# Macaron block on one core: the first pass starts after a short setup, the other weight transposes stand inside its steps, and the slot products are summed in PSUM one step later

## The chip, the core and the metric

The kernel runs on one core of one Trainium2 chip. The metric is the device time of one execution in microseconds (us). The engines are the tensor engine (PE; PEld is its weight load), the vector engine (DVE), the activation engine (ACT), GpSimd (POOL) and the sync engine (SP), whose queue issues nearly all transfers (SPq in the rows). Everything is float32.

## What is computed

The input x has the shape (2, 4096, 512). Two half-weight "slot" feed-forward blocks (with the same weights) stand around one gated delta-rule attention:

```
x = x + 0.5 * ffn(layernorm(x))
x = x + attn(layernorm(x))
x = x + 0.5 * ffn(layernorm(x))

ffn(x):                                # x already normalised; S = 64 slots, D = 512
  S      = slot_init * slot_scale
  h      = gelu([x, mean(S)] @ w1.T + b1)                # 1024 -> 256
  logits = (h @ w2.T + b2) / (|tau| + 0.1)               # 256 -> 64 slots
  alpha  = softmax over the 8 largest logits, 0 elsewhere
  gi     = (alpha.T @ x) / (sum_t alpha + 1e-8)          # over all 4096 tokens of a batch
  h_new  = GRU(gi, S; wih, whh, bih, bhh)
  return (alpha @ (h_new @ wv.T + bv)) @ wo.T + bo
```

The sum over all tokens of `alpha.T @ x` must be complete before the first block can return anything, so the kernel needs a pass over all tokens before the attention pass can begin.

## The kernel before

The tokens are cut into NT = 32 tiles of 128 tokens per batch row; a step works on one tile of each of the B = 2 rows (b = 0, 1). Each engine has its own instruction stream in program order, and semaphores (`wait_ge`, `then_inc`) are all that ties them; the order within a stream is written out by hand. The program has five parts.

**Setup.** SP loads the constants and the weights. 31 weight blocks of 128 rows (`jobs`: w1, w2, wo, wih, whh; one more job turns the slots `hs`) are loaded into four ring buffers, turned by four transposes each on PE (L625) and moved from PSUM by ACT (L1109, L1112). Then PE makes the 12 products of the slots with whh (`gh_part`, L315), which DVE adds to `gh` (L1528), the mean of the slots (L634) from which DVE makes the bias `h_bias` (L1531 to L1535), and the product of wv with wo (L639, `voT_at`) with its bias (L643, `bvo`). DVE also makes the masks (L1513 to L1524), scales w_out (L1503) and adds biases (L1504), spreads bv (L1508). All of it is done before `ready` is given (after L1546). The turned wih and the product are also stored in DRAM scratch (`wih_dram`, `vo_dram`) for the second use.

**First pass** (`pass1_pe`, `pass1_dve`, ACT's loop of `route_*`). Per step n, DVE takes the moments of tile n + 2 (L1552, L1554), POOL makes the reciprocal deviation (L1337, L1332), DVE normalises (L1563); PE turns the tile (L649), ACT moves it (L1116), PE computes the hidden layer (`route_hidden`, L662), ACT applies gelu (L1126), PE makes the logits (`route_logits`, L672), DVE finds the top 8 (`top_of`, L1569 to L1575), ACT takes exp (L1132), DVE makes alpha (`weights_of`, L1580 to L1584), PE multiplies alpha with the tile and with a column of ones (`route_slots`, L683, L684), turns alpha (L686) for ACT to move (L1137) and SP to store. DVE adds the two products to `slotacc` (`route_sums`, L1596, L1597). The logits of step n wait for ACT's move of step n - 1 (`aT`), the products of step n for DVE's sum of step n - 1 (`sacc`). Each batch row has one buffer for x (`xin`), loaded again when the normalisation has read it.

**First middle** (`mid`, `mid_dve_part`): the GRU, then the slot values `sv`. **Main pass**: first block's output, attention, routing of the second block, three steps deep; this takes most of the time and the change leaves it as it is. **Second middle and tail**: the GRU again, then the second block's output is added to the 32 tiles kept on the chip (L1921) and stored.

## Time and profile before

| | us |
|---|---|
| median of 3 runs | 3365.73 (3364.14 to 3366.76) |
| the profiled execution, its own time | 3365.4 |
| span of its instructions | 3363.2 |
| setup, to the issue of the first load of x | 82.5 |
| from there to the first transpose of the first middle | 320.1 |
| from there to the first transpose of the second middle | 2886.4 |
| from there to the end | 74.2 |
| PE busy over the span | 2867.8 (85%) |
| mean granted PE clock | 0.938 |

The profiled execution's own time is 2.2 us longer than its span and agrees with the median of the runs within 0.4 us. The middle rows come from looking at the trace in windows; the first two together, 402.6 us, are what the change touches.

### The profile page before, as it was taken

What the parts mean: (1) busy time and instruction counts of PE and PEld (TensorE: products, weight loads), DVE (VectorE), ACT (ScalarE), POOL (GpSimd) and SP (SyncE); (2) the same over time, 40 slices, a digit from 0 to 9 for tenths busy, and PEclk for the clock granted to TensorE, in tenths of its full rate; (3) what the DMA queues carried; (4) which work ended last, traced back from release to release, by engine and by line L of the source; (5) the groups of instructions that cost most, each with busy time, mean ns of one, the idle gap of its engine ahead of it and who ended that gap; (6) DMA issues with size and microseconds to landing.
All of it is one profiled execution on the core that took longest, in us unless ns stands there. A gap on an engine that the chain in (4) does not pass through costs nothing.

```text
span 3363.2 us, 121625 instructions
## 1 busy us (share of the span) xinstructions
PE 2867.8 (85%) x52954; PEld 2001.7 (60%) x52954; DVE 1965.6 (58%) x5371; ACT 948.1 (28%) x1662; POOL 1211.3 (36%) x1576
## 2 busy tenths in 40 slices
PE   6888778889898888989888888889898888989857
PEld 4666546566665666656566666666665666656643
DVE  2777645556565565656566665666666656655535
ACT  2555412222222222222222222222222222222210
POOL 0111034444443444434443434344443444434400
PEclk9999989999999998999999999999999999999968
DMA  7211112222221221112222222222222221212157
GB/s 253 68 64 58 45 33 53 54 54 54 54 54 48 54 52 37 50 46 53 54 54 54 54 54 54 54 54 54 54 54 54 54 54 52 54 44 54 47 196 288
DMA packets 365984, 225.07 MB, mean 67 GB/s; under 512 B 277584, under 2 KB 294032, under 8 KB 365456
## 3 DMA queue, kind: packets, MB, share of 16 engines
q1 hardware_dynamic: 356240, 200.51, 21.7%
q10 hardware_dynamic: 9216, 16.78, 1.3%
q8 instruction: 421, 6.90, 0.9%
q14 instruction: 107, 0.88, 0.1%
HBM read 125.49 MB, written 74.97 MB: 60 GB/s over the span
## 4 chain that ended last, share of the span: by engine, by line
PE 49%; DVE 33%; issue 10%; DMA 4%; SPq 2%; ACT 0%; POOL 0%; DVEq 0%; POOLq 0%; ACTq 0%
DVE blk L1764 12%; DVE blk L1766 11%; PE psum L752 8%; PE psum L926 4%; PE psum L835 4%; PE psum L906 4%; PE psum L883 4%; PE psum L853 4%; PE psum L893 4%; DMA xin<-in_L_attn_x_dram 3%; PE psum L797 3%; PE psum L820 2%; PE psum L866 2%; PE psum L954 2%; PE psum L746 2%
## 5 line engine op out<-in xcount | busy, mean ns | idle before, releaser
L752 PE MATMUL psum<-w_kvqg,xnT 128*128 128x512 f32 x1536 | 727.1, 607 | 3.8 <-DVE gt L1689 1.9
L1332 POOL TENSOR_TENSOR sm<-sm,half 128x1 f32<-128x1 f32 (+1 forms) x384 | 517.5, 1348 | 491.5 <-DVE sm L1791 204.9
L1764 DVE TENSOR_TENSOR blk<-blk 128x30 f32<-128x30 f32 (+14 forms) x960 | 377.8, 394 | 83.9 <-issue 51.9
L752 PEld LDWEIGHTS psum<-w_kvqg,xnT 128*128 128x128 f32 x1536 | 270.6, 191 | 253.7 <-issue 226.2
L1766 DVE TENSOR_TENSOR blk<-blk 128x30 f32<-128x30 f32 (+14 forms) x960 | 377.7, 393 | 33.0
L797 PE MATMUL psum<-xnT,w_kvqg 128*128 128x128 f32 x2048 | 300.5, 309 | 0.0
L797 PEld LDWEIGHTS psum<-xnT,w_kvqg 128*128 128x128 f32 x2048 | 290.2, 224 | 16.6 <-issue 16.6
L1354 POOL TENSOR_SCALAR sm<-sm 128x1 f32<-128x1 f32 x64 | 14.5, 227 | 788.1 <-DVE sm L1674 788.1
L926 PE MATMUL psum<-w_out,gate 128*128 128x512 f32 x512 | 269.3, 651 | 2.7 <-issue 1.2
L1782 DVE STREAM_TRANSPOSE st<-psum 128x128 f32<-128x128 f32 x256 | 80.8, 316 | 278.6 <-PE psum L906 278.4
L1162 ACT ACTIVATE xn<-xc,sm 128x512 f32<-128x512 f32 x64 | 52.1, 813 | 655.1 <-POOL sm L1358 655.1
L906 PE MATMUL psum<-qg,st 32*32 32x64 f32 x8192 | 181.0, 219 | 34.3 <-issue 31.1
L906 PEld LDWEIGHTS psum<-qg,st 32*32 32x32 f32 x8192 | 140.6, 107 | 116.3 <-issue 115.5
L954 PE MATMUL psum<-w2T,hT 128*128 128x64 f32 x256 | 60.7, 415 | 172.6 <-DVE xc L1666 171.9
L835 PE MATMUL psum<-kqT 32*32 32x64 f32 x8192 | 154.5, 218 | 45.6 <-issue 45.4
L893 PE MATMUL psum<-pk,uw 32*32 32x64 f32 x8192 | 173.4, 217 | 21.6 <-issue 21.4
L883 PEld LDWEIGHTS psum<-pk,uw 32*32 32x32 f32 x8192 | 132.5, 105 | 98.8 <-issue 94.7
L883 PE MATMUL psum<-pk,uw 32*32 32x64 f32 x8192 | 173.6, 218 | 20.3 <-issue 18.7
L835 PEld LDWEIGHTS psum<-kqT 32*32 32x32 f32 x8192 | 127.2, 106 | 106.0 <-issue 101.7
L954 PEld LDWEIGHTS psum<-w2T,hT 128*128 128x128 f32 x256 | 55.6, 319 | 196.8 <-issue 195.9
L1776 DVE TENSOR_TENSOR qg<-psum,qa 128x512 f32<-128x512 f32 x64 | 44.3, 692 | 200.2 <-ACT qg L1219 200.2
L853 PE MATMUL psum<-vk,E 32*32 32x64 f32 x8192 | 142.8, 219 | 16.1 <-issue 11.0
(266 smaller groups left out, 4912.9 us busy)
## 6 DMA issues: line engine op xcount, KB each, us to landing
xin<-in_L_attn_x_dram SPq DMA_DIRECT2D x128, 256.0 KB, 2.9
blk<-n_scratch SPq DMA_DIRECT2D x64, 512.0 KB, 4.9
n_scratch<-nn SPq DMA_DIRECT2D x64, 256.0 KB, 3.3
xh<-xc SPq DMA_DIRECT2D x64, 256.0 KB, 2.5
e_scratch<-blk SPq DMA_DIRECT2D x32, 512.0 KB, 2.6
E<-e_scratch SPq DMA_DIRECT2D x64, 256.0 KB, 4.3
x_scratch<-xh SPq DMA_DIRECT2D x62, 256.0 KB, 4.7
alphaT_scratch<-aT_out SPq DMA_DIRECT2D x64, 64.0 KB, 2.6
```

Of the source, the lines that this page charges most:

```text
L752: last = mm(dst, xnT[b][:, k * P:(k + 1) * P], w_kvqg[:, (k * 4 + m) * D:(k * 4 + m + 1) * D], start=(k == 0), stop=(k == KC - 1))
L797: last = mm(g_at[b][:, hb * P:(hb + 1) * P], w_kvqg[:, at:at + P], xnT[b][:, k * P:(k + 1) * P], start=(k == 0), stop=(k == KC - 1))
L835: last = mm(q32(gram_at[b], c, h * 2 * HD, 2 * HD), q32(kqT[b], c, h * 2 * HD, HD), q32(kqT[b], c, h * 2 * HD, 2 * HD), start=True, stop=True)
L853: last = mm(q32(uw_at[b], c, h * 2 * HD, 2 * HD), q32(E[b], c, h * HD, HD), q32(vk[b], c, h * 2 * HD, 2 * HD), start=True, stop=True)
L883: last = mm(q32(gq_at[b], hq, (hb * NC + c) * 2 * HD, 2 * HD), q32(uw[b], c, at + HD, HD), q32(pk[b], c, at, 2 * HD), start=False, stop=Tr ...
L893: last = mm(q32(y_at[b], hq, (hb * NC + c) * 2 * HD, 2 * HD), q32(uw[b], c, at, HD), q32(pk[b], c, at, 2 * HD), start=(hb % 2 == 0 and r = ...
L906: last = mm(q32(y_at[b], hq, at, 2 * HD), q32(st[b], hq, x * P + hb * HD, HD), q32(qg[b], hq, at, 2 * HD), start=False, stop=True, skip_gr ...
L926: last = mm(wo_at[b], gate[b][:, k * P:(k + 1) * P], w_out[:, k * D:(k + 1) * D], start=(k == 0), stop=(k == KC - 1))
L954: last = mm(lg_at[b], hT2[b][:, j2 * P:(j2 + 1) * P], w2T[:, j2 * NS:(j2 + 1) * NS], start=(j2 == 0), stop=(j2 == 1))
L1332: return g.tensor_tensor(dst, a, half[:, 0:n], ALU.pow)
L1764: own(tt(o, Y[:, 0:rows, s_:s_ + 1].to_broadcast([P, rows, cols]), N[:, s_:s_ + 1, s_ + 1:CH].to_broadcast([P, rows, cols]), ALU.mult))
L1766: ins = tt(Y[:, 0:rows, s_ + 1:CH], Y[:, 0:rows, s_ + 1:CH], o, ALU.add)
```

## The change

The setup is cut to what the first step needs: w1, w2, the slots, their mean and the hidden bias. The other 29 jobs (`START` onwards) stand one per step in the steps 1 to 29 of the first pass; the 12 whh products in the steps 19 to 30; the four parts of the product of wv with wo in the steps 7, 9, 11, 13 and its bias in step 15. DVE's scalings move into the steps 4 to 8. SP loads the remaining constants before step 1 and the attention weights in its turn of step 3, and writes the scratch in its turn of step 20. x gets two buffers per batch row (`xp`) and the normalised tile four (`rx`); moments and normalisation are taken three steps ahead.

`route_slots(n - 1)` now stands in PE's step n; its products go to one PSUM bank that keeps summing over all steps. The product with the ones, `route_sums` and `sacc` are gone; POOL sums alpha instead (`route_alpha`) and one product with ones at the end gives the sum. The tail waits for the reloaded tiles in pairs. On the names and the schedule:

```diff
@@ -248,21 +250,28 @@
             jobs.append((whh[j * P:(j + 1) * P, :], P, KC, ("whh", j)))
         NJ = len(jobs)
         HSJ = [j for j in range(NJ) if jobs[j][3][0] == "hs"][0]
-        rings = [kn[0], kn[1], qs[0], qs[1]]
-        tps = [A[0], A[1], Bk[0], Bk[1]]
+        rings = [xc[0], xc[1], xh[0], xh[1]]
+        tps = [Bk[0], Bk[1], A[1]] + [A[1]] * (NJ - START)
         hsT = gate[0]
         whh_ring = [gate[1], dr[0]]
-
+        rx = [xn, qs, scr, sq]
+        xp = [rxn, xin]
+        VALUE_STEP = {7 + 2 * k: k for k in range(KC)}
+        BIAS_STEP = 15
+
+        def job_of(n):
+            return START + n - 1 if START + n - 1 < NJ else None
+
+        def whh_of(n):
+
+            r = n - 1 - (HSJ + 1 - START + 1)
+            return r if 0 <= r < 12 else None
 
         wih_region = [(kqT[0], 2), (kqT[1], 2), (qg[0], 2), (qg[1], 2), (uw[0], 2), (uw[1], 2)]
         RELOAD = 16 * (len(wih_region) + KC)
 
...
```

On SP:

```diff
+            load(b1c, b1.rearrange("(j p) -> p j", p=P))
+            load_job(2)
+            load(taut, tau.partition_broadcast(P))
+            load(b2s[:, :], b2.partition_broadcast(P))
+            load_x(2)
+            load_x(3)
+            load_x(4)
+            for j in range(START, START + 2):
+                load_job(j)
+            load_rest()
+            for n in range(1, NT + 2):
+                j = job_of(n + 2)
+                if j is not None:
+                    load_job(j)
+                if n + 4 <= NT:
+                    load_x(n + 4)
+                if n == 3:
+                    load_weights()
+                if n >= 2:
+                    store_at(0, n - 2, n - 1)
+                if n == NT // 2 + 4:
+                    sp.wait_ge(wt_ev, HSJ)
+                    m = 0
+                    for buf, cols in wih_region:
+                        sp.dma_start(wih_dram[:, m * D:(m + cols) * D], buf[:, :]).then_inc(wih_st, 16)
+                        m += cols
+                    sp.wait_ge(vo_ev, KC)
```

On PE:

```diff
+            def value_part(k):
+                if k == 0:
+                    pe.wait_ge(ldb, LDB)
+                    pe.wait_ge(wt_ev, START + 4)
+                else:
+                    pe.wait_ge(vo_ev, k)
                 for e in range(KC):
-                    last = mm(ST[k % 2][:, :], wvn[e][:, k * P:(k + 1) * P], woT_at(e), start=(e == 0), stop=(e == KC - 1))
+                    last = mm(vo_at, wvn[e][:, k * P:(k + 1) * P], woT_at(e), start=(e == 0), stop=(e == KC - 1))
+                last.then_inc(vo_ps, 1)
...
-            def route_slots(j, n, src):
-
-                if j is None:
-                    pe.wait_ge(sacc, n - 1)
+            def route_slots(n):
                 for b in range(B):
                     pe.wait_ge(S["al"], both(n, b))
-                    al = alpha[:, b * NS:(b + 1) * NS]
-                    mm(A[0][b * NS:(b + 1) * NS, :], al, src[b][:, :], start=True, stop=True)
-                    last = mm(A[1][b * NS:(b + 1) * NS, 0:1], al, ones[:, 0:1], start=True, stop=True)
-                last.then_inc(sl_ps, 1)
-                tr(Bk[0][:, 3 * P:4 * P], alpha[:, :], ident[:, :]).then_inc(aT_ps, 1)
-
-            def pass1_pe(n, odd, more):
-
-                route_logits(None, n)
-                if more:
-                    route_xT(None, n + 1, C, rx[1 - odd])
-                    route_hidden(None, n + 1, ST)
-                route_slots(None, n, rx[odd])
-
+                    mm(A[0][b * NS:(b + 1) * NS, :], alpha[:, b * NS:(b + 1) * NS], rx[n % 4][b][:, :],
+                       start=(n == 1), stop=True, skip_group_check=True).then_inc(sl_ps, 1)
+                if n >= NT - 1:
+                    pe.wait_ge(aT, n - 1)
+                tr(aTr_at, alpha[:, :], ident[:, :]).then_inc(aT_ps, 1)
+
+            pe.wait_ge(set_pool, 1)
+            for j in range(START):
+                turn_job(j)
+            pe.wait_ge(set_dve, 1)
+            mm(C[0][:, :], aT_in[0:NS, :], hs[0:NS, :], start=True, stop=True).then_inc(set_pe, 1)
+            pe.wait_ge(wt_ev, START)
             pe.wait_ge(ready, 1)
-            route_xT(None, 1, C, rx[1])
-            route_hidden(None, 1, ST)
-            for i in range(1, NT // 2):
-                pass1_pe(2 * i - 1, 1, True)
-                pass1_pe(2 * i, 0, True)
-            pass1_pe(NT - 1, 1, True)
-            pass1_pe(NT, 0, False)
+            route_xT(1)
+            route_hidden(1)
+            for n in range(1, NT + 1):
+                if n < NT:
+                    route_xT(n + 1)
+                if job_of(n) is not None:
+                    turn_job(job_of(n))
+                route_logits(n)
+                if n < NT:
+                    for b in range(B):
+                        pe.wait_ge(S["rxnT"], both(n + 1, b))
+                if n > 1:
+                    route_slots(n - 1)
+                if whh_of(n) is not None:
+                    gh_part(whh_of(n))
+                if n in VALUE_STEP:
+                    value_part(VALUE_STEP[n])
+                if n == BIAS_STEP:
+                    value_bias()
+                if n < NT:
+                    route_hidden(n + 1)
```

On ACT:

```diff
+            route_move_x(1)
+            for n in range(1, NT + 1):
+                route_gelu(n)
+                if n < NT:
+                    route_move_x(n + 1)
+                if job_of(n) is not None:
+                    move_job(job_of(n))
+                route_exp(n)
+                if n > 1:
+                    route_aT(n - 1)
+                if n in VALUE_STEP:
+                    move_value(VALUE_STEP[n])
```

On POOL:

```diff
+            def route_alpha(n):
+                pl.wait_ge(S["al"], both(n, 1))
+                if n > 1:
+                    pl.wait_ge(sums1, n - 1)
+                g.tensor_tensor(sums[:, :], sums[:, :], alpha[:, :], ALU.add).then_inc(sums1, 1)
+
+            pl.wait_ge(set_dve, 1)
+            for n in range(1, 4):
+                for b in range(B):
+                    rstd(b, n, "rbn", "rrs")
+            for n in range(1, NT + 1):
+                if n + 3 <= NT:
+                    rstd(0, n + 3, "rbn", "rrs")
+                route_alpha(n)
+                if n + 3 <= NT:
+                    rstd(1, n + 3, "rbn", "rrs")
```

On DVE (the last four lines are the tail):

```diff
+            def set_gates():
+                ve.wait_ge(ldb, LDB)
+                own(tt(gh[:, 0:2 * D], gh[:, 0:2 * D], bhh_t[:, :], ALU.add))
+
+            def set_out(k):
+                own(ts(w_out[:, k * D:(k + 1) * D], w_out[:, k * D:(k + 1) * D], gcol[:, k:k + 1], 0.5, ALU.mult, ALU.mult))
+
+            def set_values():
+                for k in range(KC):
+                    own(ts(bvx[:, k * P:(k + 1) * P], ones[:, :], bv_c[:, k:k + 1], None, ALU.mult))
+                ve.nop().then_inc(set_dve, 1)
+
+            def add_gates(r):
+                ve.wait_ge(gh_ps, r + 1)
+                tt(gh[:, r * P:(r + 1) * P], gh[:, r * P:(r + 1) * P], gh_at, ALU.add).then_inc(gh_ev, 1)
+
+            def add_values():
+                ve.wait_ge(set_pe, 2)
+                own(tt(bvo[:, :], vo_at, bo_t, ALU.add))
+                own(ts(bvo[:, :], bvo[:, :], 0.5, None, ALU.mult))
...
-            def route_sums(n):
-                ve.wait_ge(sl_ps, n)
-                tt(slotacc[:, 0:D], slotacc[:, 0:D], A[0][:, :], ALU.add)
-                tt(slotacc[:, D:D + 1], slotacc[:, D:D + 1], A[1][:, 0:1], ALU.add).then_inc(sacc, 1)
...
+            for b in range(B):
+                route_normalise(1, b)
+            set_bias()
+            for n in (2, 3):
+                for b in range(B):
+                    route_moments(n, b)
+                for b in range(B):
+                    route_normalise(n, b)
+            for n in range(1, NT + 1):
                 route_top(n)
-                if more:
+                if whh_of(n) is not None:
+                    add_gates(whh_of(n))
+                if n == BIAS_STEP:
+                    add_values()
+                if n + 3 <= NT:
+                    route_moments(n + 3, 0)
+                route_weights(n)
+                if n + 3 <= NT:
+                    route_moments(n + 3, 1)
                     for b in range(B):
-                        route_moments(n + 2, xin, b)
-                route_weights(n)
-                route_sums(n)
-                if more:
-                    for b in range(B):
-                        route_normalise(n + 2, xin, rx[odd], b)
-
-            ROUTE = 2 * (1 + 1 + 1 + 1 + 1 + 3)
-            for n in (1, 2):
-                for b in range(B):
-                    if n == 2:
-                        ve.wait_ge(S["rxn"], both(1, b))
-                    route_moments(n, xin, b)
-                    route_normalise(n, xin, rx[n % 2], b)
-            for i in range(1, NT // 2):
-                pass1_dve(2 * i - 1, 1, True)
-                pass1_dve(2 * i, 0, True)
-            pass1_dve(NT - 1, 1, False)
-            pass1_dve(NT, 0, False)
+                        route_normalise(n + 3, b)
+                if n == 4:
+                    set_gates()
+                    set_values()
+                if 5 <= n < 5 + KC:
+                    set_out(n - 5)
...
-                if i < NT - 1:
-                    ve.wait_ge(x2_in[i], 16 * B)
+                if i % 2 == 0:
+                    ve.wait_ge(x2_in[i // 2], 16 * B * (2 if i + 2 < NT else 1))
```

How the streams stand, at three places. First PE, one step of the first pass before; `qs` or `xn` is the normalised tile, `kn` the hidden layer:

```order
L672 MATMUL psum<-w2T,kn 128x64 x4
L649 MATMUL psum<-ident,qs 128x128 x8
L662 MATMUL psum<-xnT,w1T 128x128 x16
L683 MATMUL psum<-xn,alpha 64x512
L684 MATMUL psum<-ones,alpha 64x1
L683 MATMUL psum<-xn,alpha 64x512
L684 MATMUL psum<-ones,alpha 64x1
L686 MATMUL psum<-ident,alpha 128x128
```

And one of the steps 19 to 29 in the changed kernel, where the weight transposes (L633) and a whh product (L640) stand:

```order
L618 MATMUL psum<-ident,sq 128x128 x8
L633 MATMUL psum<-ident,xh 128x128 x4
L691 MATMUL psum<-w2T,kn 128x64 x4
L698 MATMUL psum<-qs,alpha 64x512 x2
L702 MATMUL psum<-ident,alpha 128x128
L640 MATMUL psum<-dr,gate 128x128 x4
L681 MATMUL psum<-xnT,w1T 128x128 x16
```

The slot products moved from behind the hidden layer to ahead of it, and take the alpha of the step before.

Second DVE, from the last alpha of a step to the first instruction of the next step, with what each waits for, before:

```order
L1584 TENSOR_SCALAR alpha<-lgt,sm 128x64 [waits aT_ps,dve_own]
L1596 TENSOR_TENSOR slotacc<-slotacc,psum 128x512 [waits sl_ps]
L1597 TENSOR_TENSOR slotacc<-slotacc,psum 128x1
L1563 TENSOR_SCALAR qs<-xin,sm 128x512 [waits rrs] x2
L1569 SCALAR_TENSOR_TENSOR lgt<-psum,itau,b2s 128x64 [waits lg_ps]
```

And in the changed kernel:

```order
L1638 TENSOR_SCALAR alpha<-lgt,sm 128x64 [waits sums1,aT_ps,dve_own]
L1601 BN_STATS sm<-rxn 128x6 [waits xe_in1]
L1603 BN_AGGR sm<-sm 128x2 [waits dve_own]
L1614 TENSOR_SCALAR xn<-rxn,sm 128x512 [waits sl_ps,rrs] x2
L1620 SCALAR_TENSOR_TENSOR lgt<-psum,itau,b2s 128x64 [waits lg_ps]
```

The two sums that waited for this step's products (`sl_ps`) are gone; the moments of batch row 1 stand there, directly ahead of the normalisation that needs them, and that one waits for products of an earlier step.

Third SP, the transfers that stand ahead of the first use in the changed kernel (the loads into `xin` and `rxn` are tiles of x):

```order
L389 DMA xc<-in_L_ffn_w_dram 128x512 x2
L377 DMA hs<-in_L_ffn_slot_init_dram 64x512 x2
L377 DMA sm<-in_L_ffn_slot_scale_dram 64x1 x2
L395 DMA xin<-in_L_attn_x_dram 128x512 x2
L377 DMA blk<-in_L_ffn_w_dram 128x2x512
L377 DMA rxT<-in_L_ffn_b_dram 128x2x1
L389 DMA xh<-in_L_ffn_w_dram 64x256
L377 DMA sm<-in_L_ffn_tau_dram 128x1
L377 DMA b2s<-in_L_ffn_b_dram 128x64
L395 DMA rxn<-in_L_attn_x_dram 128x512 x2
```

Before, 20 loads of constants of 4.6 MB stood ahead of the first wait of DVE, and no tile of x was loaded before `ready`; now 8 loads and the first tile stand there.

## Rows read from the trace of the kernel before

**Rows 1.** Windows: us, busy time of each engine, granted clock, DMA share, GB/s.

```profile
0.00:82.47 82.47, 51.02 (x264) 34.85 (x264) 22.15 (x58) 22.44 (x81) 1.08 (x8) 1.00 0.77 257
82.47:402.56 320.09, 259.87 (x1824) 207.05 (x1824) 229.48 (x900) 181.32 (x352) 50.51 (x128) 0.97 0.19 60
```

**Rows 2.** Timeline, one step, DVE: start, us, instruction, idle before it and its releaser.

```profile
202.00 0.28 DVE L1569 SCALAR_TENSOR_TENSOR lgt<-psum,itau,b2s 128x64 f32<-128x64 f32 x1
...
204.93 0.69 DVE L1552 BATCH_NORM_STATS2 sm<-xin 128x6 f32<-128x512 f32 x1 [0.17 <-DVE lgt L1575]
...
206.85 0.19 DVE L1580 TENSOR_TENSOR lgt<-lgt 128x64 f32<-128x64 f32 x1
...
208.41 0.26 DVE L1584 TENSOR_SCALAR alpha<-lgt,sm 128x64 f32<-128x64 f32 x1
...
209.89 0.69 DVE L1596 TENSOR_TENSOR slotacc<-slotacc,psum 128x512 f32<-128x512 f32 x1 [1.23 <-PE psum L684]
...
210.56 1.00 DVE L1563 TENSOR_SCALAR xn<-xin,sm 128x512 f32<-128x512 f32 x2
```

**Rows 3.** Timeline, the same step, PE.

```profile
201.01 1.10 PE L672 MATMUL psum<-w2T,kn 128*128 128x64 f32 x8 [0.37 <-ACT aT_out L1137]
...
203.25 3.84 PE L662 MATMUL psum<-xnT,w1T 128*128 128x128 f32 x32 [0.25 <-ACT xnT L1116]
...
207.93 1.43 PE L683 MATMUL psum<-xn,alpha 128*64 128x512 f32 x3 [0.85 <-DVE alpha L1584]
...
210.48 1.10 PE L672 MATMUL psum<-w2T,kn 128*128 128x64 f32 x8 [0.37 <-ACT aT_out L1137]
```

**Rows 4.** Timeline, the first step's normalisation of batch row 0, DVE.

```profile
87.47 0.55 DVE L1563 TENSOR_SCALAR qs<-xin,sm 128x512 f32<-128x512 f32 x1 [1.13 <-POOL sm L1332]
```

**Rows 5.** Timeline, the same step, ACT.

```profile
203.70 1.28 ACT L1132 ACT_TABLE_LOAD   x1
...
205.00 0.59 ACT L1132 ACTIVATE lgt<-lgt,sm 128x64 f32<-128x64 f32 x2
```

**Rows 6.** Timeline, DVE in the setup, and PE's first transpose of batch row 1.

```profile
22.17 0.49 DVE L1491 TENSOR_SCALAR hs<-hs,sm 128x512 f32<-128x512 f32 x1 [22.17 <-DMA w_out<-in_L_attn_Wo_dram]
...
24.76 2.05 DVE L1503 TENSOR_SCALAR w_out<-w_out,gcol 128x512 f32<-128x512 f32 x4
26.85 1.23 DVE L1504 TENSOR_TENSOR gh<-qa,blk 128x1024 f32<-128x1024 f32 x1
...
29.03 1.25 DVE L1508 TENSOR_SCALAR xin<-ones,sq 128x128 f32<-128x128 f32 x4
...
33.52 0.18 DVE L1524 TENSOR_SCALAR eye<-qa 128x32 f32<-128x32 int32 x1
...
61.53 0.69 DVE L1531 COPY scr<-psum 128x512 f32<-128x512 f32 x1 [1.28 <-PE psum L634]
...
65.15 0.16 DVE L1535 TENSOR_TENSOR h_bias<-sm,sq 128x2 f32<-128x2 f32 x1
...
90.66 1.12 PE L649 MATMUL psum<-ident,qs 128*128 128x128 f32 x4 [1.42 <-DVE qs L1563]
```

**Rows 7.** Chain that ended last: start, us, what (L315 whh product, L639 wv times wo).

```profile
50.10 0.89 PE psum L315 x8
...
61.49 13.95 PE psum L639 x32
```

**Rows 8.** Tile sums, main pass: duration ns min/median/max; first and last start.

```profile
L1433 POOL TENSOR_TENSOR sums<-sums,alpha x32: 452/453/460, 648.8 to 3283.2; 128x128 f32<-128x128 f32 x32
```

**Rows 9.** DMA issues of the setup: KB each, median us from issue to landing.

```profile
w_kvqg<-in_L_attn_Wg_dram SPq DMA_DIRECT2D x1, 1024.0 KB, 12.1
```

**Rows 10.** Tile xin in the first pass, the loads of x.

```profile
DMA to landing us min/median/max: 2.5/2.8/4.8
```

**Rows 11.** Timeline, last step's first instruction of DVE, and the first middle's first transpose.

```profile
393.33 0.28 DVE L1569 SCALAR_TENSOR_TENSOR lgt<-psum,itau,b2s 128x64 f32<-128x64 f32 x1 [0.53 <-PE psum L672]
...
402.56 1.11 PE L345 MATMUL psum<-ident,gate 128*128 128x128 f32 x4 [2.06 <-DVEq L1633]
```

428 lines of the change are left out of this document (193 added, 235 removed).

## Prediction, made before the changed kernel was run

> **What bounds the kernel now.** I looked first at the windows by part. The setup takes 82.5 us with PE busy for 51 and DVE for 22, and the first pass 320.1 us with PE busy for 260, DVE for 229, ACT for 181 [rows 1]: in neither is an engine full. The main pass (2886 us) is not touched, so only these 402.6 us and the tail are in play. Then I read one step of the first pass in the timeline. It repeats every 9.47 us (the logits at 201.01 and at 210.48) [rows 3]. On DVE the step is a chain without air: two top-8 searches 2.93 (202.00 to 204.93), two moments 1.92, two alphas 1.82 (206.85 to 208.67), then 1.23 of waiting for PE's slot products, the sums, two normalisations 1.00, and at once the next top-8 [rows 2]. On PE the logits and the transposes take 2.0 (201.01 to 203.25 less 0.25 of waiting), the hidden layer 3.84, then it waits for alpha, and the slots with their turn fill 207.93 to 210.48 [rows 3]. So each engine waits in turn for the other through alpha, and DVE is the one that comes nearest to being full.
>
> **The start.** DVE's first wait ends at 22.17, on transfers of 4.6 MB, and the first pass has both tiles ready for PE at 90.66 [rows 6]. Now 2.0 MB stand ahead of that wait. Transfers take at least 2.5 us to land [rows 10]; scaling the rest, (22.2 - 2.5) x 2.0 / 4.6 + 2.5 gives 11.1. What DVE then does before `ready`: hs and the tau chain, part of the 2.6 between 22.17 and 24.76, I take 1.6; two moments 1.9 [rows 2]; the masks 3.4 (30.28 to 33.70); two normalisations 1.0; the bias 3.8 (61.53 to 65.31) [rows 6]. Sum 11.7, so PE starts the first tile at 22.8 instead of 90.66: **-67.9 us**. Everything else of the setup must be paid inside the pass.
>
> **The step on DVE.** Removed: the wait of 1.23 and the two sums, 0.67 (209.89 to 210.56) [rows 2]. Added: the moments of row 1 now stand right ahead of the normalisation, whose reciprocal POOL makes after them, a wait of 1.13 [rows 4]; the normalisation of row 0 lies inside it, that of row 1 (0.55) behind. So the step is 2.93 + 1.92 + 1.82 + 0.06 (the sums' place) + 1.13 + 0.55 = 8.41, with the handover 8.45. POOL's new sum of alpha is 0.45 [rows 8] and is done before those moments are; it costs nothing, and 0.45 per step if it were not. The top-8 no longer waits for ACT's move of alpha.
>
> It would cost more if POOL's sum held DVE up while it runs: then 0.45 in each of the 32 steps, 14 us. The 32 equal sums of the main pass run beside a DVE that is over half busy and take 452 to 460 ns each [rows 8], so nothing there is stretched. The Trainium skill, SBUF — State Buffer, section Who interferes with whom, has a rule that speaks against this place: a DVE instruction in a two-port mode, or with two SBUF inputs, and a GpSimd instruction that reads SBUF lock each other out for a whole instruction. By that rule the 14 us would be the worst case; the trace does not show it.
>
> **The step on PE.** Logits and transposes 2.0, hidden layer 3.84, four slot passes of 512 columns at 13.95 / 32 = 0.436 each [rows 7] 1.75, alpha's turn 0.14 by estimate (a pass as in the whh product is 0.11), and the job's four transposes 0.44 (half of the 8 passes of 0.89) [rows 7]: 8.15 us. In the steps 19 to 29 the whh product adds 0.89: 9.04; DVE's added 0.29 or so is hidden there. Each of the five parts of wv times wo adds eight passes, 3.49 [rows 7]: 11.64, and nothing covers that, except the lead that PE has over DVE (some 2.3 us in step 7 and 9). The alpha of step n - 1 is ready 5.8 us after its top-8 began, some 2 us or more before PE asks for it.
>
> **The step on ACT.** Two table loads of 1.28 [rows 5], the moves, gelu, exp (busy 181.3 over 32 steps is 5.7 each [rows 1]) and about 0.7 for the job: 6.4 us, below both.
>
> **The sum.** The first tile's fill (transposes, move, hidden layer, at the lower clock as before) is some 6.5, and DVE's first top-8 comes 2.4 later (transposes 1.0, job 0.4, logits until DVE 1.0): 31.7. Steps 1 to 8 go by DVE: 8 x 8.45 = 67.6, plus its moved work 2.05 + 1.23 + 1.25 = 4.5 [rows 6]; the value part of step 7 hides in PE's lead. That is 103.8. Steps 9 to 15 go by PE: 4 x 11.64 + 3 x 8.15 - 2.3 = 68.7; 16 to 18 by DVE 25.4; 19 to 29 by PE 99.4; 30 (no job) 8.6; 31 (no job, no product) 7.7; step 32 needs no next tile, -1.4. DVE's first instruction of step 32 is then at 312.2, instead of 393.33 [rows 11]. From there to the first middle 9.2 us before; the last product of the ones comes behind it (+0.7), a memset of 0.5 leaves that stretch: 9.4. The middle starts at 321.6 instead of 402.56: **-81.0**. Against that I set 3 us of losses at handovers and for loads of x that come late. The tail waits in pairs on tiles that landed long before; 0. Main pass 0. So 3365.4 - 78 = **3287 us**. Sum and medians are within 0.4 us, so the same number stands for the median.
>
> **The transfers.** SP issues in order. The load of x for step n + 4 can go once step n - 1 is normalised and is needed one and a half steps later, about 11 us; it lands in 2.8, at most 4.8 [rows 10]. Behind a block of weights it is another thing: the last of the four 1 MB weights took 12.1 us to land [rows 9], and SP's queue is itself held up while it issues them. Three blocks stand ahead of loads of x now: the rest of the constants before step 1 (3.8 MB), the attention weights in step 3 (4 MB), the scratch in step 20 (4 MB). A block that held SP for 8 us and the load for 12 would eat the 11 and cost 9. I expect the first two to cost 0 to 3 each.
>
> **Rivals.** (1) The block transfers starve the pass: two or three times 5 to 9 us, so 3294 to 3311, mid 3301. For it: 12.1 in [rows 9]; against: those four MB were issued at once when the engines were already busy with others. (2) The steps do not get shorter, since each engine waits in turn as before: 9.47 in steps 1 to 18 (170.5, + 4.5, + 4 x 2.2 of value parts), 9.5 in 19 to 29, 9.5 in 30 and 31: 31.7 + 170.5 + 4.5 + 8.8 + 104.5 + 19 + 9.4 = 348.4, and 3365.4 - 54 = 3311. For it: 1.9 us only leave DVE's chain, and 1.6 come in; against: the chain through alpha now has a step of slack. (3) ACT becomes the bound. If each change of tables took as long again as its load of 1.28 [rows 5], ACT would need 6.4 + 2.6 = 9.0 per step: steps 1 to 8 lose 4.4, 9 to 18 some 4, 19 to 29 nothing: 3296. In the trace the load ends at 204.98 and the next activation starts at 205.00 [rows 5], so there is no such time. The Trainium skill, ScalarE: Activation LUTs, section What ACT_TABLE_LOAD costs, gives 1283 ns for the load, as here, but a drain of 1380 ns beside it; by its figures it would be 9.2 per step and 3299. (4) POOL's sum holds DVE up in each step, as worked out above: 3301. (5) Better than the sum: DVE's wait for POOL is partly overlapped and the losses are nil: 0.3 less per DVE step and no 3 us, 3279. (6) The other side: PE runs the pass at the lower of its two clocks, 1.2 GHz, because it now starts from long idleness and waits often. The granted clock was 0.97 over the pass [rows 1], so it doesn't now. Passes would double: a step of 8.15 would be near 15, and the pass 30 x 6.5 = 195 us longer: 3480. It decides from a mean step of 11.1 us on (8.45 + 81 / 30).
>
> **How the numbers follow.** My forecast, 3280 to 3294: 0.55. Rival 1: 0.17; rival 2: 0.11; rival 3: 0.03; rival 4: 0.02; rival 5 (below 3280): 0.09; rival 6: 0.02; 0.01 for no gain by some stall that I do not see. The range takes in rivals 1 to 5 but for their ends: 3276 to 3312. A measurement of this kernel can tell 0.2%, 6.7 us; faster than that 0.97, within it 0.01, slower 0.02.
>
> **What would show it.** Right: PE's first transpose of a tile near 23 us; a step of 8.4 to 8.5 with DVE idle only ahead of the second normalisation, 1.1 us less 0.5; 9.0 in the steps 19 to 29 with PE full; 11.6 in the value steps; the first middle near 324; the stretch from there to the end 2961 as before. Wrong: DVE's moments waiting for DMA in the steps 2, 5 and 22 (rival 1); PE waiting for alpha or gelu in each step (rival 2); a gap between a table load and its activation (rival 3); the clock below 0.95 in the pass (rival 6); the main pass longer or shorter by over 3 us, for which I have no term.

## The result: 3262.4 us, faster than the range allowed

Median 3262.43 us over four runs (3255.60 to 3268.81), before 3366.24; ratio 0.9692 [0.9664, 0.972]. Predicted were 3287, in a range of 3276 to 3312. The profiled execution took 3255.6, 31.4 less than forecast. By landmarks of the two traces:

| us | before | after | gain | predicted |
|---|---|---|---|---|
| first tile on PE | 90.66 | 24.10 | 66.6 | 67.9 |
| first middle | 402.56 | 307.43 | 95.1 | 81.0, less 3 |
| first product of the main pass | 427.30 | 331.56 | 95.7 | 78 |
| second middle | 3288.99 | 3179.51 | 109.5 | 78 |
| end of the span | 3363.2 | 3253.7 | 109.5 | 78 |

Windows of the changed kernel up to the main pass (columns as in [rows 1]):

```profile
0.00:24.10 24.10, 4.49 (x13) 2.39 (x13) 10.85 (x33) 2.76 (x4) 2.78 (x12) 1.00 0.39 124
24.10:307.43 283.33, 263.46 (x1951) 219.34 (x1951) 212.70 (x854) 196.53 (x401) 68.19 (x156) 0.98 0.42 132
307.43:331.56 24.13, 18.95 (x40) 7.99 (x40) 6.18 (x10) 4.37 (x6) 0.00 (x0) 0.86 0.08 24
```

The pass holds 127 more PE records than before (1951 against 1824 in [rows 1]). From the first tile to the first middle it takes 283.3 us, where the kernel before took 311.9 (90.66 to 402.56), so it is 28.6 shorter. The timeline of DVE, one step with a whh sum (start, us, instruction, idle before it and its releaser):

```profile
237.38 0.28 DVE L1620 SCALAR_TENSOR_TENSOR lgt<-psum,itau,b2s 128x64 f32<-128x64 f32 x1
...
240.17 0.29 DVE L1580 TENSOR_TENSOR gh<-gh,psum 128x128 f32<-128x128 f32 x1
240.37 0.69 DVE L1601 BATCH_NORM_STATS2 sm<-xin 128x6 f32<-128x512 f32 x1
...
242.86 0.26 DVE L1638 TENSOR_SCALAR alpha<-lgt,sm 128x64 f32<-128x64 f32 x1
243.03 0.69 DVE L1601 BATCH_NORM_STATS2 sm<-xin 128x6 f32<-128x512 f32 x1
...
245.29 0.55 DVE L1614 TENSOR_SCALAR sq<-xin,sm 128x512 f32<-128x512 f32 x1 [0.77 <-POOL sm L1369]
245.76 0.28 DVE L1620 SCALAR_TENSOR_TENSOR lgt<-psum,itau,b2s 128x64 f32<-128x64 f32 x1
```

From top-8 to top-8 it is 8.38, and the only idle time of DVE that the timeline marks is the 0.77 for POOL. The order is that of [rows 2], with the slot sums gone. PE in a value step (one with a part of wv times wo), and in the step shown of DVE:

```profile
121.07 1.04 PE L618 MATMUL psum<-ident,xn 128*128 128x128 f32 x8
...
124.48 3.60 PE L651 MATMUL psum<-vk,pk 128*128 128x512 f32 x8
127.92 3.73 PE L681 MATMUL psum<-xnT,w1T 128*128 128x128 f32 x32
131.49 0.27 PE L618 MATMUL psum<-ident,qs 128*128 128x128 f32 x1
...
238.22 3.74 PE L681 MATMUL psum<-xnT,w1T 128*128 128x128 f32 x32
241.80 1.04 PE L618 MATMUL psum<-ident,scr 128*128 128x128 f32 x8
242.67 0.60 PE L633 MATMUL psum<-ident,xh 128*128 128x128 f32 x4
243.11 1.00 PE L691 MATMUL psum<-w2T,kn 128*128 128x64 f32 x8
244.04 1.08 PE L698 MATMUL psum<-xn,alpha 128*64 128x512 f32 x4
245.05 0.33 PE L702 MATMUL psum<-ident,alpha 128*128 128x128 f32 x1
245.21 1.06 PE L640 MATMUL psum<-gate 128*128 128x128 f32 x8
```

Four records of the slot products (L698) begin at 244.04 and the next instruction at 245.05: 1.01 for what the forecast put at 1.75. The value step is 131.49 - 121.07 = 10.42 with 3.44 of value part (124.48 to 127.92), so a plain step on PE is 6.98; with whh 7.9. The forecast had 11.64, 8.15 and 9.04. So DVE sets the plain steps and the whh steps. A value step and the plain step behind it need 17.4 on PE (10.42 + 6.98); from step 7 on these pairs take 17.8, 16.6, 16.7 and 17.4, the second and third no more than two steps of DVE, since PE has some lead there.

### The profile page after: what moved, and what is told of

It reads as the page before. It is cut to its first block, busy times and chain, and to the rows that moved or that the text cites. A ratio compares the mean times of both kernels' runs of the same rounds, so it can differ in the third digit from the quotient of the medians.

```text
span 3253.7 us, 121458 instructions
## 1 busy us (share of the span) xinstructions
PE 2816.3 (87%) x52828; PEld 1973.8 (61%) x52828; DVE 1939.1 (60%) x5299; ACT 944.0 (29%) x1634; POOL 1232.0 (38%) x1608
## 4 chain that ended last, share of the span: by engine, by line
PE 49%; DVE 32%; issue 10%; DMA 4%; SPq 2%; POOL 1%; ACT 1%; DVEq 0%; POOLq 0%; ACTq 0%
DVE blk L1823 12%; DVE blk L1825 12%; PE psum L784 8%; PE psum L958 5%; PE psum L867 4%; PE psum L938 4%; PE psum L915 4%; PE psum L885 4%; PE psum L925 4%; PE psum L829 3%; DMA xin<-in_L_attn_x_dram 3%; PE psum L852 2%; PE psum L898 2%; PE psum L986 2%; PE psum L778 2%
## 5 line engine op out<-in xcount | busy, mean ns | idle before, releaser
L915 PEld LDWEIGHTS psum<-pk,uw 32*32 32x32 f32 x8192 | 131.7, 105 | 87.1 <-issue 82.9
L925 PEld LDWEIGHTS psum<-pk,uw 32*32 32x32 f32 x8192 | 137.7, 105 | 29.3 <-issue 28.6
```

Of the source, the lines that this page charges most:

```text
L915: last = mm(q32(gq_at[b], hq, (hb * NC + c) * 2 * HD, 2 * HD), q32(uw[b], c, at + HD, HD), q32(pk[b], c, at, 2 * HD), start=False, stop=Tr ...
L925: last = mm(q32(y_at[b], hq, (hb * NC + c) * 2 * HD, 2 * HD), q32(uw[b], c, at, HD), q32(pk[b], c, at, 2 * HD), start=(hb % 2 == 0 and r = ...
```

## Experiments

Fifteen more runs: thirteen kernels with an edit, and both kernels again. T and R with a number name a theory and its rival in the expectations. "First middle" is the time of PE's first transpose there; "main pass" runs from its first product to the first transpose of the second middle. Both are from the one profiled execution of each run, the medians from all its executions.

**The transposes back in the setup.** All jobs, whh products and value parts before the first tile:

```diff
-            return START + n - 1 if START + n - 1 < NJ else None
+            return None
...
+            for j in range(START, NJ):
+                turn_job(j)
```

> The changed kernel with one part undone: all weight transposes, the whh products with their sums and the value parts stand in the setup again; the order inside a step of the first pass and the slot products summed in PSUM stay. This splits the gain of 95 us at the first middle into its two parts. Theory T1 (DVE sets every step at 8.3 us, PE has over 1 us of slack in it): without the jobs the steps cost the same 8.3, so from the first tile to the first middle I expect 283.3 (24.10 to 307.43 in the changed kernel) less the DVE work that moves out (4.5) and the 6 us of waits for transfers in steps 2 to 5, that is 272 to 279, against 311.9 before; with a first tile at about 88 to 91 the first middle is at 360 to 370, so the reordered step gives some 35 us and the moved setup some 60. Rival R1 (the steps are short for a reason that goes with the moved work, for example that the jobs keep PE busy and its clock up): without them the steps go back towards 9.47 and the middle towards 390. Time of the whole: T1 3320 to 3335, R1 3350.

First top-8 at 94.7, steps of 8.3 (but for three of 8.7 to 11.8), first middle at 360.48, median 3308.2 (ratio 0.9828 [0.9802, 0.9854]). That is 12 us below T1's 3320, most of it in the main pass (2851.8, where the kernel before has 2861.7), of which more below. T1 holds, R1 falls: the short step doesn't depend on the moved work. Of the 95 us, 42 come with the reordered step (402.56 to 360.48) and 53 with the short setup.

**The two rows' slot products kept apart.**

```diff
                 for b in range(B):
+                    if b == 1 and n < NT - 1:
+                        mm(C[0][:, P:P + 1], ident[:, :], ones[:, 0:1], start=True, stop=True)
                     pe.wait_ge(S["al"], both(n, b))
```

> The changed kernel with one more product on PE between the slot products of the two batch rows: identity times ones, one column, all 128 columns of the array, into a free corner of PSUM (steps 1 to 30). It can only start behind the first row's product and the second row's only behind it, so the two cannot run beside each other. Theory T1 (PE's step was forecast 1.1 us too long mainly since the two products of 64 columns run at the same time, 1.08 us for all four records where four passes of 0.436 make 1.75): the four take about 1.75 to 1.9 here, PE's job step grows from 7.0 to about 7.8, and DVE's pitch stays at 8.3 in the plain steps (the first middle moves by less than 4 us, all of it in the steps 19 to 29, where PE then needs 8.6 against 8.37, and the value steps). Rival R2 (the passes of a product in fp32 are shorter in general when nothing interrupts them): the records still take about 1.1 us and nothing moves. Rival R3 (PE is the bound after all): the pitch grows by the same 0.7 in all steps and the first middle by over 20 us.

PE's timeline, one step:

```profile
123.50 1.07 PE L700 MATMUL psum<-qs,alpha 128*64 128x512 f32 x2
124.50 0.38 PE L698 MATMUL psum<-ones,ident 128*128 128x1 f32 x2
124.81 1.07 PE L700 MATMUL psum<-qs,alpha 128*64 128x512 f32 x2
125.81 0.33 PE L704 MATMUL psum<-ident,alpha 128*128 128x128 f32 x1
```

One row alone takes 1.0; in the changed kernel both together take 1.01, so they run at the same time. Apart, with the small product, they take 2.31 (123.50 to 125.81), 1.3 more and not the 0.7 to 0.8 that I expected. T1's mechanism is shown, its size was wrong again: the first middle moves by 25.5 us and not by less than 4. PE's plain step becomes 6.98 + 1.3 = 8.3, near the 8.15 of the forecast, and the forecast's terms come near: steps 19 to 29 take 99.6 us (forecast 99.4, changed kernel 92.5), steps 30 and 31 15.1 (14.9, 11.7), steps 9 to 15 72.8 (68.7, 61.4). First middle 332.90, median 3302.5. Of the 45.7 us by which its profiled execution is longer than the changed kernel's, 25.5 are lost in the first pass by 30 products of one column; another 17.3 lie in the main pass (2865.2 against 2848.0 us), whose code is the same, and the last experiments below bear on that. R2 falls; of R3 only the whh and value steps are true.

**Moments of both rows first on DVE** (POOL's two roots ahead of its sum likewise):

```diff
                     route_moments(n + 3, 0)
+                    route_moments(n + 3, 1)
                 route_weights(n)
                 if n + 3 <= NT:
-                    route_moments(n + 3, 1)
```

> The changed kernel with both rows' moments on DVE ahead of the alphas, and POOL's two reciprocal roots ahead of its sum of alpha; nothing is added or left out. It takes away DVE's wait of 0.77 for POOL before the second normalisation. Theory T1 (DVE sets every step, in all of the 32): the pitch falls by the wait, from 8.3 to about 7.5 to 7.6 in the plain steps; PE's own step of 7.0 (7.9 in the steps 19 to 29, 10.4 in the five value steps) then bounds the latter two kinds, so the first middle comes 18 to 24 us earlier. Rival R3 (PE or the loop through the other engines sets the pitch): less than 5 us.

Plain steps fall to 7.6, as T1 has it, but the first middle comes at 302.12, 5.3 earlier, not 18 to 24. I had counted 0.75 in nearly every step; yet the value pairs stay at PE's 17.4 and the whh steps at its 7.9, and step 4 took 13.3 us instead of 11.6. So T1 has the plain steps right and the total wrong. Median 3254.93.

**SP's queue in another order.**

```diff
+            load_x(5)
             load_rest()
...
-                if n == 3:
-                    load_weights()
...
+                if 5 <= n < 9:
+                    load_weight(n - 5)
```

> The changed kernel with another order on SP's queue only: the load of x for tile 5 ahead of the block of constants, and the attention weights one per step in the steps 5 to 8 instead of all in step 3. DVE waited 3.31 us for x in step 2 and PE 5.1 us in step 4 for a move that waited for a store behind that block (0.44 of it reached DVE). Theory T1: the first of the two goes away, the first middle comes 2.5 to 4 us earlier, the rest as it is. Rival R4 (the transfers of the block share the engines with the loads of x, whatever the order): less than 1 us, or the same wait one tile later.

The wait for x (3.31 us in the changed kernel) is gone, as T1 has it, but the first middle comes only 1.4 us earlier (306.05, not 2.5 to 4). As in R4's second form the wait has moved: PE waits for a block of wo that SP issues behind the constants (a line of the waits of PE up to 110 us: total, times, longest).

```profile
PE psum L633 <- DMA xc<-in_L_ffn_wo_dram: 5.2, 1, 5.2
```

Windows of this kernel; the last three columns are the granted clock, the transfer engines' busy share and GB/s:

```profile
40.00:48.00 8.00, 4.31 (x37) 3.91 (x36) 6.39 (x26) 4.34 (x11) 1.92 (x5) 1.00 0.98 381
48.00:56.00 8.00, 6.37 (x29) 4.64 (x30) 4.16 (x18) 3.92 (x7) 0.49 (x3) 0.57 0.43 154
```

The transfer engines are full at 381 GB/s (371 in the same 8 us of the changed kernel). PE's wait ends at 49.6, and from 48.2 to 55.0 the granted clock is at its lower level of 1.2 GHz (0.57 of 2.4 in the mean of the second window).

**Fewer bytes early, on top of the moments.** wv in steps 3 and 4, the other constants in 5 to 8, attention weights in 9 to 12, the moved DVE work in steps 8 and 10 to 14. The edit on DVE, which stands on top of e3's:

```diff
-                if n == 4:
-                    set_gates()
+                if n == 8:
                     set_values()
-                if 5 <= n < 5 + KC:
-                    set_out(n - 5)
+                if n == 10:
+                    set_gates()
+                if 11 <= n < 11 + KC:
+                    set_out(n - 11)
```

> The kernel of e3_moments_first with its transfers in another order and the moved DVE work elsewhere; nothing is left out. x of tile 5 goes before step 1; of the block of constants the two halves of wv go in the steps 3 and 4, the rest in the steps 5 to 8, the attention weights one per step in 9 to 12; the bias values on DVE go from step 4 to 8, the sum of the gates to 10, the four scalings of w_out from 5 to 8 to 11 to 14, all into steps in which PE does value parts. Theory T3 (in e3 and e4 the wait for data only changed its place, since the block fills the transfer engines at 370 to 380 GB/s between 40 and 48 us, so it is bytes at this time that must go and not their place in the queue): steps 1 to 6 take 7.6 each, the steps 7 to 16 go in pairs of 17.4 (PE: 7.0 + 10.4), first middle at 290 to 295, that is 12 to 17 us earlier than in the changed kernel (307.4) and some 8 to 10 earlier than in e3 (302.1). Rival R5 (the 13.3 us of step 4 in e3 are a wait of the loop through alpha and not of loads): the early steps keep 3 or more of these 6 us, first middle 297 or later. Median of the whole with T3: 3240 to 3250.

Steps 1 to 6 take 7.6 to 8.0, value pairs 16.8 to 18.2, first middle 289.09. T3 holds, R5 falls: steps 1 to 6 together take 46.0 us against 56.8 in e3, and DVE work that stands elsewhere now accounts for only 3.5 of these 10.8 (1.23 + 1.25 out of step 4, a scaling of 0.5 each out of steps 5 and 6). The order of the loads and their bytes were changed together here, so it isn't shown that bytes alone did it. Median 3244.62, ratio 0.9637 [0.9623, 0.9651]: the fastest version of all.

**Slot products in their own step again.**

```diff
-                if n > 1:
-                    route_slots(n - 1)
...
                     route_hidden(n + 1)
-            route_slots(NT)
+                route_slots(n)
...
```

> The changed kernel with one part undone: the slot products and alpha's turn of step n stand in step n again, behind the hidden layer of tile n + 1, and ACT moves the turned alpha first in the next step. Summing in PSUM, the jobs in the steps and the order on DVE stay. Theory T1 (what makes the step short is that alpha has a step of slack before PE asks for it): the loop logits, top-8, moment, alphas, slots, transposes, logits closes in every step again, PE waits for alpha, and the pitch goes back to 9.2 to 9.6 in plain steps; first middle 30 to 40 us later than 307.4. Rival R6 (the shorter chain on DVE alone, the sums and their wait removed, makes the step short): pitch 8.3 to 8.6, first middle less than 10 us later.

PE's timeline:

```profile
228.86 3.74 PE L681 MATMUL psum<-xnT,w1T 128*128 128x128 f32 x32
232.58 1.95 PE L698 MATMUL psum<-sq,alpha 128*64 128x512 f32 x4
234.47 0.33 PE L702 MATMUL psum<-ident,alpha 128*128 128x128 f32 x1
235.25 1.06 PE L618 MATMUL psum<-ident,qs 128*128 128x128 f32 x8 [0.46 <-ACT aT_out L1166]
```

The pitch is 9.5 in all plain and whh steps, the 9.47 of the kernel before. That a whh product of 0.9 on PE doesn't lengthen the step shows that the loop through alpha sets it, and not PE's work. The second row's product starts at 233.46, when DVE has made its alpha (233.15 + 0.26), so the two rows no longer run side by side: 1.95 for the four. First middle 356.39, 49 later than 307.43 and not 30 to 40, since value steps (11.1) and early loads cost more too (step 3 took 18.7). T1, not R6: with the sums gone in either case, it is the step of slack for alpha that makes the step short.

**Is the rest of the gain chance?** The first product of the main pass stands 95.7 us earlier, but the median is 104 us lower. A delay at the end of the first middle, and both kernels again:

```diff
+                if m == 0:
+                    for _ in range(12):
+                        own(v.memset(sv[:, :], 0.0))
                 stt(sv[:, :], Bk[1][:, :], 0.5, bvo[:, :], ALU.mult, ALU.add).then_inc(mid_dve, 1)
```

> The changed kernel with 12 extra memsets of 128x512 of sv on DVE (about 0.48 us each) just before sv is made at the end of the first middle, where all other engines wait: a delay of 5.8 us ahead of the main pass and nothing else. Theory T2 (the main pass takes 2847 to 2865 us from one execution to another by chance, as the seven times of the kernel before on one chip, 3351 to 3373, show; the part of the changed kernel's gain that lies in the main pass is such chance): the median goes up by 6 within 6, the main pass of the profiled execution is anywhere between 2845 and 2868. Rival R7 (the length of the main pass follows from the moment at which it starts, so the 95 us of the first pass set its 13 us): the four or five times of this kernel agree within 3 us, but at a distance from 3268 that is not the delay.

> The kernel before, unchanged, once more with a profile of its own. The gain of the changed kernel is 95.7 us up to the first product of the main pass (427.3 to 331.6) and 13.7 behind it in its profiled execution; in the eight variants measured so far the rest behind that product takes 2922 to 2942 us. Theory T2 (that length is chance): the profiled execution of the kernel before has a main pass anywhere from 2845 to 2868, and the first product again within 1 us of 427.3. Rival R8 (the change really shortens the main pass by some 8 us, for example through where tiles lie, which all its variants share): 2857 or longer here and in the two kernels below.

> The changed kernel, unchanged, once more with a profile of its own, beside the kernel before. T2: its times spread over 10 us or more again, 3255 to 3272, and the main pass of the profile is anywhere from 2845 to 2868. R8: 2855 or shorter.

> The kernel before with the 12 extra memsets of sv at the end of the first middle (7.9 us in a12_delay). T2: the first product of the main pass at 435.2, times up by 8 within 6, the main pass of the profile anywhere from 2845 to 2868. R8: 2857 or longer. R7 (the length follows from the moment of the start): all its times within 3 us of each other, away from the kernel before plus 8.

> The kernel before with 4 such memsets (2.6 us). The same question: T2 the main pass anywhere from 2845 to 2868, times up by 2.6 within 6; R8 2857 or longer; R7 all its times within 3 us of each other.

| kernel | times, us | main pass, us |
|---|---|---|
| a12_delay | 3262.4 to 3279.6 | 2847.2 |
| before_again | 3358.6 to 3377.0 | 2861.8 |
| after_again | 3263.1 to 3271.2 | 2858.7 |
| b12_delay | 3365.1 to 3388.3 | 2860.1 |
| b4_delay | 3364.5 to 3377.2 | 2858.5 |

One kernel's own times spread over up to 23 us, so R7's first form (the moment of the start sets the length) falls. R8 isn't borne out whole: the kernel before and its two delayed forms are at 2858.5 to 2861.8, as it has it, but the changed kernel's second trace is at 2858.7 and not at 2855 or shorter. Still only variants of the changed kernel have come down to 2847, so T2 as the whole story is doubtful as well.

What differs between the two kernels is where PE stops. Among the small 32x32 products it stops again and again with no releaser. Kernel before, timeline, and two windows: their PE counts are the matmul records up to the main pass's first product and ahead of the stop.

```profile
554.96 0.47 PE L835 MATMUL psum<-kqT 32*32 32x64 f32 x18 [1.98 <-issue]
```

```profile
0.00:427.30 427.30, 330.45 (x2129) 250.24 (x2129) 257.81 (x968) 208.12 (x439) 51.60 (x136) 0.97 0.30 96
0.00:554.91 554.91, 426.53 (x3853) 314.17 (x3853) 318.26 (x1111) 233.94 (x478) 103.56 (x187) 0.94 0.26 81
```

The changed kernel, the same two views:

```profile
464.16 0.48 PE L867 MATMUL psum<-kqT 32*32 32x64 f32 x20 [2.22 <-issue]
```

```profile
0.00:331.50 331.50, 286.89 (x2002) 229.72 (x2002) 229.67 (x896) 203.65 (x411) 70.97 (x168) 0.97 0.39 124
0.00:464.11 464.11, 384.25 (x3819) 294.01 (x3819) 291.19 (x1042) 230.69 (x452) 124.08 (x223) 0.94 0.32 98
```

The second trace of each kernel has these two stops at the very same counts (3853; 3819). A first stop of 3.0 to 3.7 us, 62 to 64 records behind the first product in every kernel, is left out here. All other stops of over 1.15 us in the main pass, in each of the 17 traces, lie on one grid of 125.74 matmul records, within 5 records. Behind the first product the two stops shown stand at 1724 records before (3853 - 2129) and at 1817 after (3819 - 2002). Four kernels move the grid by products in the first middle that nothing reads (two matmul records each):

```diff
+                if m == 0:
+                    for _ in range(16):
+                        mm(ST[0][:, 0:1], ident[:, :], ones[:, 0:1], start=True, stop=True)
                 e.wait_ge(mid_dve, o_dve + 6)
```

> The kernel before with 16 products of one column (identity times ones, 32 matmul records) on PE in the first middle, behind its third gate product, where PE waits for 3 us; nothing reads them. Theory T4 (PE's program reaches it in blocks of about 126 matmul records, and the stops of 1.3 to 2.5 us come where a block ends among small products; what counts is where the blocks' ends lie against the main pass): the stops lie at the same absolute counts modulo 126 as before, so 32 records earlier against the start of the main pass, which is where the changed kernel has them (1438, 1689, 1817, 4581, 4834 records behind the first product, within 3): the same pattern of steps as the changed kernel (the first 89 83, the last 80) and a main pass of 2847 to 2858. Rival R7 (something else of the change): stops as before it, main pass 2858 to 2862, the last step 90.

> The changed kernel with 46 such products (92 records, some 5 us more in the first middle, which is not counted here). T4: the stops move to where the kernel before has them against the first product (1723, 2602, 2980, 4993), the last step takes 88 to 91, main pass 2857 to 2863. R7: the changed kernel's pattern, the last step 80, main pass 2847 to 2858.

> The kernel before with 63 such products (126 records, one whole block). T4: the pattern of the kernel before comes back whole, with the last step at 90 and a main pass of 2858 to 2862. Rival R9 (any added product changes the pattern, whatever their number): another pattern.

> The kernel before with 32 such products (64 records, half a block). T4: the stops 64 records earlier against the first product than before (1659, 2538, 2916 and so on where they fall among small products), a pattern of steps that is neither of the two; its main pass I can't say beforehand, between 2845 and 2870. It shows how much this position is worth. R7: pattern and length of the kernel before.

b_shift16, the windows of the same two places:

```profile
0.00:427.62 427.62, 332.25 (x2161) 253.66 (x2161) 257.96 (x968) 208.07 (x439) 51.76 (x136) 0.98 0.30 96
...
0.00:560.59 560.59, 430.89 (x3980) 318.98 (x3981) 319.33 (x1113) 235.19 (x480) 106.01 (x192) 0.95 0.26 81
```

The stops of over 1.3 us up to some 5000 records behind the first product (exact to three records), the last step (from the last but one to the last move of the gates, `gt<-psum` on ACT), the main pass of the profiled execution, and the median of all executions:

| kernel | stops behind the first product | last step | main pass | median |
|---|---|---|---|---|
| before | 1724, 2603, 2981, 4994 | 90 | 2861.7 | 3366.2 |
| b_shift63 | 1727, 2606, 2984, 4997 | 88 | 2859.3 | 3386.5 |
| a_shift46 | 1725, 2604, 2982, 4996 | 88 | 2861.6 | 3279.7 |
| after | 1438, 1689, 1817, 4204, 4581, 4834 | 81 | 2848.0 | 3262.4 |
| b_shift16 | 1440, 1692, 1819, 4206, 4584, 4836 | 81 | 2851.3 | 3357.0 |
| b_shift32 | 1032, 1410, 1788, 3423, 4175, 4553 | 83 | 2874.8 | 3374.6 |

T4 holds where it was definite, R7 and R9 fall: the kernel before with 32 records more takes on the pattern of the changed one, the changed one with 92 more that of the kernel before, and 126 more change nothing. The steps follow: over the 32 stretches from one step's first product to the next, two traces with the same stops differ by 30 to 55 us (differences summed without sign), one with the stops of before and one with those of after by 126 to 155. b_shift16 is faster than the kernel before though it only adds work: 3357.0 against 3368.6 on the same chip, ratio 0.9968 [0.9954, 0.9982]. Two sizes were missed. The 46 products of a_shift46 put the main pass's first product 15.3 us later and not 5, and b_shift32's 2874.8 lies outside 2845 to 2870. But that profiled execution is the slowest of its kernel's eleven (3390.6, median 3374.6), so 2874.8 is not the usual length of its main pass.

Over the traces the main pass takes 2858.5 to 2861.8 with the stops of before (six traces, mean 2860.5) and 2847.1 to 2858.7 with those of after (nine, mean 2851.8): 8.7 us. The first 31 stretches take the same in the mean (2656.1 and 2656.4); the whole difference lies in the last one, 204.4 against 195.5. e2 and b_shift32 have stops of their own and stand outside both groups. The other executions agree with this: each one's time, less what its kernel's trace has outside the main pass, gives an estimated mean of 2861.7 (46 executions) and 2853.7 (41), 8 us apart. What splits the nine into 2847 to 2852 and 2857 to 2859, with nearly the same stops, stays open.

What the stops are can be read from the transfers. The page of the kernel before lists a queue of the kind "instruction" (packets, MB, share):

```profile
q8 instruction: 421, 6.90, 0.9%
```

Each of its packets moves 16384 bytes. PE's 52954 matmuls and as many weight loads, divided by 421, are 251.6 instructions or 125.8 matmul records per packet, the spacing of the stops; in the changed kernel it is 52828 records to 420 packets, the same 125.8. All of the 852 stops of over 1.15 us in the 17 traces end 1.2 to 1.7 us behind the end of such a packet; of moments drawn at random in the main pass 8% stand so. So PE stops because its next block of instructions comes late. How the place of these stops makes the last stretch 9 us shorter or longer has not been followed up.

## Why the prediction was too careful

- **The start**: 24.10 against 22.8, first top-8 33.3 against 31.7. The scaling of bytes was 1.2 short (first wait to 12.27 instead of 11.1).
- **"8.45 on DVE"**: right in kind and nearly in size, 8.3. The wait for POOL was 0.77 instead of 1.13 less the hidden row.
- **Steps 1 to 8, 72.1**: 75.1, of it 3.3 for x in step 2. That is the mild form of rival 1, which the 3 us of losses were for; the full form didn't come, though the transfer engines are full from 40 to 48 us.
- **"Four slot passes of 512 columns at 0.436 each 1.75"**: the first step that failed. The price was taken from products that use all 128 columns; these use 64 each, and the two rows run together, 1.01. With the hidden layer (3.58 until the next begins, not 3.84) and logits and transposes (1.80, not 2.0) shorter as well, PE's step was forecast 1.17 too long. Steps 9 to 15: 61.4 instead of 68.7; 19 to 29: 92.5 instead of 99.4, since DVE bounds them; 30 and 31: 11.7 instead of 14.9. That is 17.4 us. e2 is the counter-proof: with 1.3 us more on PE per step the steps 19 to 31 take what was forecast, and 9 to 15 take 4 more.
- **"A memset of 0.5 leaves, the last product comes behind"**: 8.2 instead of 9.4.
- Sum up to the first middle: + 1.6 + 3.0 - 7.3 - 0.1 - 6.9 - 3.2 - 1.2 = -14.1 (321.6 to 307.43), and the 3 us of losses on top lay in it already.
- **"Main pass 0"**: the second step that failed. 13.7 in the profiled execution, 8.7 in the mean of the traces, by the place of PE's stops for instructions, for which no term and no range stood. The prediction named a change of over 3 us here as something that it had no term for. The range ended at 3276; without these 8.7 the median would be 3271, so the first failed step alone puts it outside.
- Rivals: 2 would be true without the later slots (e7 shows its 9.5). 3 fell: the next activation follows the table load at once (231.72 + 1.28, then 233.01). The Trainium skill, ScalarE: Activation LUTs, section What ACT_TABLE_LOAD costs, has a drain of 1380 ns there; the trace does not show it. Rival 4 fell: DVE's moments take 0.69 beside POOL's sum (0.46, from 243.20) as they do without it. The Trainium skill's rule in SBUF — State Buffer, section Who interferes with whom, is not put to the test by that: it has no lock for a DVE instruction with one SBUF input outside the two-port modes, and nothing here shows the moments in such a mode. Rival 6: the clock was 0.98 over the pass.
- Rival 5 was in the right direction, at 3279 and with 0.09, but for another reason (the wait for POOL and the losses). PE's step, made of a sum of busy times with nothing for overlap, erred to the long side here.

## What to carry to other kernels

Where two engines wait for each other once per step, move one product a step later before making anything shorter: with the sums already gone, 9.5 became 8.3 by that. Price products by a row with the same columns and the same neighbours: two of 64 columns each, when both are ready at once, cost one. And when a part whose code is unchanged becomes a few per mille longer or shorter, count the instructions ahead of it before believing in either gain or loss: 16 added products that nothing reads made the kernel before 11.6 us faster here. And compare many executions: one kernel's own spread over up to 23 us, and a single profiled one can be the slowest of them.

## What was unexpected of the hardware

- **PE stops at fixed counts, for its instructions.** The stops in the groups of small products are of 1.3 to 2.8 us, one near the end of the main pass of 2.8 to 4.5; over the main pass PE's idle time put down to issue in its four groups of small products is 113 us before. The Trainium skill, Runtime: NRT & Kernel Launch, section Instruction fetch mechanics, says that an engine's instructions arrive in blocks of 256 and that crossing a block's end is mostly hidden. The traces agree with the blocks (251.6 recorded instructions per packet of 16384 bytes); that crossing is hidden does not hold here among small products. Why the blocks come late there is not shown.
- **Two products of 64 columns at once.** 1.01 us together, 1.0 for one alone (e2). The Trainium skill, TensorE: Matmul & The Clock Gate, section Part 3: Packing small matmuls — row/col tiling, describes it, and the traces agree. In the kernel before the two products hardly meet: the second row's starts at 208.72, when its alpha is there (208.41 + 0.26), and the first row's began at 207.93. It is the step of slack that lets them run together.
- **A wait on PE brings the lower clock.** In e4 a wait of 5.2 us, up to 49.6, went with 6.8 us at 1.2 GHz (48.2 to 55.0): a mean granted clock of 0.57 from 48 to 56, against 0.79 in the changed kernel, where that wait was 1.3. The changed kernel has a wait of 5.1 us of its own, up to 69.4, and is at 1.2 GHz from 66.4 to 73.2.
